# Nine token groups of two layouts instead of eight of one, a second group summed on TensorE, and the work at the two ends of the first stage moved

## The reference

```python
h      = concat(patches(x) @ W + b, txt)           # [32, 333, 192]
q      = layernorm(h)
key    = grouped_pointwise(depthwise(q, 9 taps))   # per head
kern   = softmax((key * q) @ ak + ak_b)            # 12 heads x 9 taps
h      = h + sum_k kern[..., k] * value[t + k - 4] # the window
xn     = layernorm(h)
top2   = two largest of xn @ Wg                    # place in the expert, in token order
out    = h + sum over the two kept experts of weight * ffn_e(xn)
```

## Time and profile before

| | |
|---|---|
| median of three runs | 1454.35 us |
| the profiled execution's own time | 1453.47 us |
| its span, first to last instruction | 1451.7 us |
| PE busy, share of the span | 1202.5 us, 83% |
| DVE busy | 1019.9 us, 70% |
| POOL busy | 691.9 us, 48% |
| ACT busy | 464.8 us, 32% |
| first instruction of stage 2 | 815.1 us |
| first product of the experts | 839.0 us |

### The profile page before, as it was taken

How to read it: one execution, slowest core, us unless ns; L and a number is a source line. 1 busy time by engine, 2 the same in 40 slices (tenths; PEclk the granted TensorE clock), 3 DMA queues, 4 the chain that set the end, 5 groups by cost and what they waited for, 6 DMA issues and landing times. The chain is left out here.

```text
span 1451.7 us, 30799 instructions
## 1 busy us (share of the span) xinstructions
PE 1202.5 (83%) x8700; PEld 1012.9 (70%) x8701; DVE 1019.9 (70%) x2367; ACT 464.8 (32%) x1197; POOL 691.9 (48%) x530
## 2 busy tenths in 40 slices
PE   6987998997989898951642089999999999999995
PEld 6766777775767777640422078988898898898895
DVE  4117959999999999999586366666666666666663
ACT  1111222333222232311113344444444444444442
POOL 1000221656656666754647724554545454545454
PEclk9999999898989998975675589999999999999998
DMA  9995554565646363548611446544444444444442
GB/s 306 402 318 138 141 166 106 161 177 163 169 114 208 104 180 85 160 100 219 191 46 48 124 61 64 68 56 62 61 63 57 63 58 63 57 63 59 61 60 28
DMA packets 215171, 175.31 MB, mean 121 GB/s; under 512 B 121864, under 2 KB 198694, under 8 KB 215104
## 3 DMA queue, kind: packets, MB, share of 16 engines
q1 hardware_dynamic: 170128, 115.36, 32.5%
q0 software_dynamic: 34720, 34.38, 14.5%
q10 hardware_dynamic: 10256, 24.73, 4.6%
HBM read 69.24 MB, written 88.47 MB: 109 GB/s over the span
## 5 line engine op out<-in xcount | busy, mean ns | idle before, releaser
L1238 POOL DMA_INDIRECT out<-yb,meta x182 | 298.0, 1638 | 313.4 <-DMA out<-yb,meta 204.0
L129 POOL DMA_INDIRECT expert_inputs<-slot_rows,slots x176 | 237.9, 1351 | 85.6 <-issue 60.2
L1023 PE MATMUL bankK<-normedT,conv_w 128*128 128x333 f32 x864 | 274.0, 465 | 0.0
L1308 DVE TENSOR_TENSOR hidden<-silu,bankU 128x256 f32<-128x256 f32 x364 | 153.3, 421 | 141.7 <-PE bankU L1346 94.3
L1264 ACT ACTIVATE silu<-bankG 128x256 f32<-128x256 f32 x364 | 139.8, 384 | 304.6 <-PE bankG L1346 304.6
L1023 PEld LDWEIGHTS bankK<-normedT,conv_w 128*128 128x128 f32 x864 | 167.1, 199 | 76.2 <-issue 9.4
L1359 PE MATMUL bankY<-expert_weights,hidden_high 128*128 x728 | 179.2, 246 | 0.8
L1360 PE MATMUL bankY<-expert_weights,hidden_high 128*128 x728 | 179.3, 246 | 0.0
L1361 PE MATMUL bankY<-expert_weights,hidden_low 128*128 x728 | 179.1, 246 | 0.0
L713 DVE TENSOR_TENSOR prod<-window_values,kb 128x960 f32<-128x960 f32 (+1 forms) x135 | 167.9, 1253 | 3.6
L731 DVE TENSOR_TENSOR hidden_group<-hidden_group,prod 128x960 f32<-128x960 f32 (+1 forms) x135 | 169.1, 1252 | 0.5
(11 more groups left out here) (162 smaller groups left out, 2295.2 us busy)
## 6 DMA issues: line engine op xcount, KB each, us to landing
patches<-in_x SPq DMA_DIRECT2D x16, 1536.0 KB, 8.5
expert_inputs<-prod ACTq DMA_DIRECT2D x6, 3430.0 KB, 23.3
token_rows<-rowbuf SPq DMA_DIRECT2D x32, 492.0 KB
window_values<-token_rows SPq DMA_DIRECT2D x32, 264.0 KB, 5.4
hidden_group<-token_rows SPq DMA_DIRECT2D x32, 264.0 KB, 7.1
window_values<-token_rows SPq DMA_DIRECT2D x32, 192.0 KB, 5.7
kb<-token_rows SPq DMA_DIRECT2D x32, 148.5 KB, 4.6
token_rows<-rowbuf SPq DMA_DIRECT2D x32, 148.0 KB
```

The costliest lines, as they stand in the source:

```text
L129: nc.gpsimd.indirect_dma_start(out=xslots[:, :], out_offset=bass.IndirectOffsetOnAxis(ap=idx[g % 2][:, k, r:r + 1], axis=0), in_=xrow[g % ...
L1023: mm = T_.matmul(bankK[(u + t) % 2][:, 0:L], conv_w[:, t // 2, k, :], qT[u][:, t, k:k + L], start=(k == 0), stop=(k == K - 1))
L1238: nc.gpsimd.indirect_dma_start(out=out[:, :], out_offset=bass.IndirectOffsetOnAxis(ap=meta[t % NMETA][:, c, 0:1], axis=0), in_=yb[v][:, c, ...
L1308: V.tensor_tensor(hf[j % 2][:, :], sg[j % 2][:, :], bankU[j][:, 0:TS], ALU.mult)\
```

## The change

- Groups have layouts of their own. Group 0 is pair 0 and group 8 is pair 15, two images each, six tokens per partition (64 partitions for each image, slices of three and three tokens). Groups 1 to 7 are pairs 1 and 2, 3 and 4, up to 13 and 14, with eleven tokens as before. The loop becomes one pair, then seven iterations of two pairs, then one pair; in each iteration the window of the group before and the routing of the one before that stand as they did.
- The tail holds groups 7 and 8, both with their first slice summed by PE. Pair 15's attends stand ahead of it, with eight pieces of group 6's window behind each of the first two.
- A group of six tokens has 12 scatters. In the tail the order on POOL is new, and the first part of the scatters of groups 6 and 7 is 15 instead of 7. The last group's scatters are cut six and six.
- The six fills are issued one at a time in iterations 1 and 2, out of buffers of their own; DVE waits for none of them.
- `EARLY` is 2 and a new `MIDDLE` is 5: experts 0 and 1 are split in stage 1, 2 to 4 at the beginning of stage 2, 5, 6 and 7 between its first tiles; PE waits for five, and for one more at each of tiles 5, 6 and 7. SP issues the loads of experts 6 and 7 behind the loads of tiles 0 and 1.

```diff
-SLICES = [(0, 6), (6, R)]
+GROUPS = [_group([0], 6, [(0, 3), (3, 6)])]
+GROUPS += [_group([p, p + 1], 11, [(0, 6), (6, 11)]) for p in range(1, NPAIR - 1, 2)]
+GROUPS += [_group([NPAIR - 1], 6, [(0, 3), (3, 6)])]
...
-EARLY = 4
+EARLY, MIDDLE = 2, 5
+LAST_FIRST = 6
...
-            SC_AT = (0, 7, TOPK * R)
+            def sc_at(g):
+                if g == NG - 3:
+                    return 0, 15, nsc(g)
+                if g == NG - 2:
+                    return 0, 15, nsc(g)
+                return 0, nsc(g) // 3, nsc(g)
...
+                low_parts(NG - 3, 1)
+                scatter(NG - 3, 0)
+                slice_norm(NG - 2, 0)
+                slice_norm(NG - 2, 1)
                 low_parts(NG - 2, 0)
-                scatter(NG - 3, 0)
-                slice_norm(NG - 2, 1)
                 scatter(NG - 3, 1)
                 low_parts(NG - 2, 1)
-                scatter(NG - 2, 0)
                 slice_norm(NG - 1, 0)
                 slice_norm(NG - 1, 1)
+                scatter(NG - 2, 0)
                 low_parts(NG - 1, 0)
+                low_parts(NG - 1, 1)
                 scatter(NG - 2, 1)
...
-                for r in range(R):
-                    scatter_rows(NG - 1, r, last_sent)
+                for n in range(LAST_FIRST):
+                    scatter_rows(NG - 1, n, last_sent)
...
-                        if g == 0:
-                            dve.wait_ge(fill_done, 16 * NFILL)
...
+                f, g, h = NG - 1, NG - 2, NG - 3
+                for t in range(2):
+                    attend(NPAIR - 1, t)
+                    part(8)
+                attend(NPAIR - 1, 2)
                 part(2 * NSL * K)
                 softmax_top(g)
                 softmax_end(g)
...
+                for k in assisted(g):
                     if k == 3:
                         top_two(h)
-                    if k == 6:
+                    if k == 4:
                         offsets(h)
                         places(h)
+                    if k == K:
+                        softmax_top(f)
+                softmax_end(f)
+                for k in assisted(f):
+                    if k == K:
+                        top_two(g)
+                        offsets(g)
+                        places(g)
+                top_two(f)
+                offsets(f)
+                places(f)
...
+            SPLIT_AT = {1: MIDDLE, 3: E - 2, 5: E - 1}
...
-                for e in (E - 2, E - 1):
-                    load_w(sp, e, raw_of(e), w_loaded[2])
...
+                            load_w(sp, E - 2 + t, raw_of(E - 2 + t), w_loaded[2 + t])
...
-                        pe.wait_ge(w_low, E)
+                        pe.wait_ge(w_low, max(MIDDLE, t + 1))
```

More of the change, by code:

```diff
@@ L582, in _ @@
+                scores_out(0)
+                for it in range(1, NG - 1):
+                    a, b = GROUPS[it].pairs
+                    normalise(b)
+                    if it < 3:
+                        fill(3 * it - 3)
+                    exponentials(it - 1)
+                    tiles_out(b)
+                    scores_out(a)
+                    if it < 3:
+                        fill(3 * it - 2)
                     if it > 1:
                         normalise_slice(it - 2, 1)
-                    if it > 1:
-                        routing_out(it - 2, 0, NQ)
@@ L1027, in conv @@
                         if k in at:
-                            next(beside)
+                            next(beside, None)
                 def values(p, c):
@@ L1100, in _, with attention @@
                 pe.wait_ge(conv_w_ready, 1)
-                for it in range(NG):
-                    p, h = 2 * it, it - 2
-                    router = logits(h, p + 1) if it > 1 else None
+                def attention(p, router=None):
                     for t in range(3):
-                        conv(p, t)
+                        conv(p, t, router, ((), (1, 3, 5), (1, 3, 5, 7))[t] if router else ())
                         values(p, t)
-                    transposes(p + 1)
+                    if not last(p):
+                        transposes(p + 1)
@@ L1121, in _ @@
-                    if p + 3 < NPAIR:
-                        patch(p + 3)
-                    if it > 1:
-                        counts_before(h)
-                    for c in range(3):
-                        scores(p + 1, c)
-                g, h = NG - 1, NG - 2
-                for _ in logits(h, NPAIR):
+                for it in range(NG):
+                    for p in GROUPS[it].pairs:
+                        h = it - 2
+                        routes = h >= 0 and not last(p) and p == GROUPS[it].pairs[-1]
+                        attention(p, logits(h, p, p) if routes else None)
+                        if routes:
+                            counts_before(h, p)
+                        for c in range(3):
+                            scores(p, c)
@@ new lines, in summed @@
+                def summed(g, steps=None):
+                    hgf = hg[g % 2][:, :, :].rearrange("p r d -> p (r d)")
+                    wait(pe, sum_out, TAIL.index(g))
+                    pe.wait_ge(hg_loaded[g % 2], loads(g, "hg"))
+                    for b, n in enumerate(columns(g)):
+                        T_.matmul(bankL[b][:, 0:n], idn[:, :], hgf[:, b * 512:b * 512 + n], start=True, stop=False)
+                    for k in range(K):
+                        pe.wait_ge(tap_made, K * TAIL.index(g) + k + 1)
+                        for b, n in enumerate(columns(g)):
+                            mm = T_.matmul(bankL[b][:, 0:n], idn[:, :], prodL[k % 2][:, b * 512:b * 512 + n],
+                                           start=False, stop=(k == K - 1))
+                        mm.then_inc(tap_summed, 1)
+                        yield k
@@ L1147, in _ @@
-                counts_before(g)
+                for k in summed(g):
+                    if k == 3:
+                        counts_before(h, NPAIR)
+                router = logits(g, NPAIR, NPAIR)
+                for k in summed(f):
+                    if k > 4:
+                        next(router)
+                for _ in router:
+                    pass
+                counts_before(g, NPAIR)
+                for _ in logits(f, NPAIR, NPAIR):
+                    pass
+                counts_before(f, NPAIR)
```

608 lines of the change are left out of this document (319 added, 289 removed).

## The result

The changed kernel takes 1469.4 us (median of four runs, 1466.7 to 1469.8), the kernel before in the same comparison 1454.0 (1453.7 to 1456.0): a ratio of 1.0099, interval 1.0085 to 1.0112. The forecast was 1437 us. The profiled execution has a span of 1467.7 us.

A forecast was written before the change was run, and what follows sets the result against it. DVE paces stage 1, a chain across engines the tail, TensorE stage 2. First product at 816.1 plus 618.7 us of stage 2 gives a span of 1434.8, by the median's offset 1437 us; range 1424 to 1451.

The forecast's parts named there:

- Step (1): Start until pair 15: six fills cost 6 us in all; pair 15's attend at 616.6 instead of 621.4, gaining 4.8 us.
- rival (c): Iterations 1 and 2: fills in flight delay stores, text and window loads, 6.7 us each; 1471 us, slower; chance 0.06.
- Step (2): Tail, pair 15 to the last statistics: 113.3 us of work and 15.7 idle, 129.0 instead of 136.4.
- Step (3): Last statistics to the change of stage: POOL's work ends at 792.5, stage 2 begins at 797.1 instead of 815.1 us.
- Step (4): Change of stage to first product: six scatters, not 11, then the tile's load; 19.0 us instead of 23.9.
- Step (5): Stage 2: 612.7 us plus 3 for three moved splits and 3 for tile 1's late load, 618.7 us.
- Rival (d): POOL's 28 scatters before the change of stage take 2.26 us each, not 1.27; 1464 us, slower; chance 0.03.
- Rival (b): Stage 2: three splits paid in full (16.8 us) and tile 1 waits 9; 1457 us, no change; chance 0.05.

The follow-up runs named there:

- run 2: The changed kernel with its fills moved: two behind normalise(1), one behind each of normalise(2) to normalise(5), none beside a pair's store: 1454.2 us, ratio to before 0.9943.
- run 11: The changed kernel with the zeros behind the images' rows written by one transfer over all 32 images instead of three: 1465.5 us, ratio to before 1.0008.
- run 8: The changed kernel measured again, unaltered, in a later comparison with the kernel before: 1469.7 us, ratio to before 1.0048.
- run 3: The changed kernel with ACT's exponential of group 0 behind pair 2's tiles instead of ahead of them: 1468.5 us, ratio to before 1.0036.
- run 12: kernel 5 with SP's zero wait behind the first store, one zero transfer behind images, one fill behind each of normalise(1) to (4), two behind (5): 1445.0 us.
- run 6: kernel 5 with the part on stage 2 undone, four experts split in stage 1 and all splits before the first product: 1453.7 us, ratio to before 0.9951.
- run 7: The kernel before with only the change's part on stage 2 (expert splits and weight loads) added: 1462.7 us, ratio to before 0.9997.
- kernel 5: The changed kernel with SP issuing the zero transfers, fills placed as in run 2, group 0's exponential behind pair 2's tiles: 1449.7 us, ratio to before 0.9921.

## Why the prediction was wrong

The path of the forecast was right, until pair 15, the tail and stage 2 in a row; its first term was not, and it turned a gain into a loss.

**Step (1), the start, failed,** in three ways that the runs took apart. First, it gave the six fills 6 us in all; other places for them give 15 us back (run 2), which two stores had lost that each have a fill issued half a microsecond ahead. This is the mechanism of rival (c), which stood at 0.06. Its price for a colliding fill was too low (6.7, where 9.5 and 9.8 us are lost at pairs 3 and 5) and its count too high: two fills collide, not six. That its 1471 us lie so near the 1469.4 measured is chance; the zeros and the exponential make up the difference. What I had against it, "20 us of room for a store", counted the room until the buffer's next use; but a store beside a fill takes 14 us instead of 6, and DVE stands at it ahead of the statistics that PE's next pair waits for. Second, "Pair 1 stays at 69.1" left out the zero transfers: the diff makes three into five, and two more DMAs on ACT's queue were priced at nothing, though ACT's first normalise is behind them. They cost 4 to 6 us (run 11 against 8, across two comparisons); at pair 0 it is 3 us in run 8's profile and 7 in the first. Third, the exponential of group 0 went ahead of the tiles of pair 2: 3.4 us there (run 3). The order on ACT shows it; I had looked for such a swap only in the tail.

**That the first term's plan can be met without these** is shown by run 12, with 101.0, 134.2, 168.5 and 213.4 against 100.2, 134.3, 168.4 and 212.9 forecast for pairs 2 to 5, and 618.7 against 616.6 for pair 15. In part this is luck: the plan has 3 us for a fill in each of two pairs, and run 12 has no wait for a store there.

**Step (2), the tail:** 134.6 and 135.1 us in the changed kernel and run 12, 129.0 forecast. The exponential waits 2.25 (1.5 forecast) and PE's sums 9.67 (11): the exchange of the two waits was as forecast. The waits of DVE over 0.3 us sum to 17.3 us (15.7 forecast): one of 4.15 for group 7's gate was not in the sum, and the two sums to copy, put at 1.6 each, show none. What is left, 117.3 us, was put at 113.3; these 4 us of work stay open.

**Step (3)** gave 51.5 us from the last statistics to stage 2: 52.5 and 53.3. **Step (4)** 19.0 to the first product: 19.3 and 19.4, released by the tile's load. **Step (5)** 618.7 us for stage 2: 616.8 and 616.6. Rival (d) did not come: the scatters of the last groups are 1.28 us apart but for those beside DVE's splits. Rival (b) did not: the splits cost 3.4 by run 6, where the forecast had 3 for them and 3 for tile 1.

**Open:** why the kernel before took 1454 us in one comparison and 1461 to 1464 in the others, while the changed kernel stayed. The profile of run 7, which has its stage 1, has the attend of pair 15 at 621.0 as before, and then loses: PE stands for over 4 us from 638 on, amid the gate's products, with nothing in the trace that releases it, the last statistics come 8.5 us later than in the kernel before (766.3 against 757.8), and stage 2 some 6. One profile doesn't tell whether that is it.

## What to carry to other kernels

Give each DMA that an edit adds or moves three prices: the issue on its engine's queue and who is behind it there, the engines it spreads over, and which transfer that someone waits for is under way beside it. A large transfer off the critical path belongs where the next awaited one is at least its own landing time away (11 to 20 us for the fills of the changed kernel), and a queue with nothing urgent behind it should issue it. And when a plan of times pair by pair exists, the first row that departs from it names the cause sooner than any total.

## What the runs showed of the hardware

A DMA's issue took 0.4 us in the middle of the loop and 10.84 for 960 KB behind the other zeros (7.12 in another execution of the same kernel, 6.85 behind one transfer over all images), and what stands behind it on the issuing engine waits, ACT's computing included. On SP a load of patches behind the zeros took 21.5 us to issue (kernel 5). A store of 1280 KB beside a fill of 3430 KB landed 14 us after its issue instead of 6, though the two are on different queues. The Trainium skill ("DMA: Bandwidth & Descriptors", section "Queues, rings and completion order") says that a DMA's semaphore write lands only after every earlier write of that DMA engine, across its queues; this would do it, and no run here tells it from plain sharing of bandwidth. TensorE's granted clock was at 0.50 of full (1.2 GHz) from 32 to 40 us in the changed kernel; TensorE had stood idle from 27.9 to 35.8. From 42 us on it was 1.00 again.
